# A Mamba-2 mixer with a gated stream mixer: pieces for the norm multiply, CB one slot later, and another order at both ends of the output passes

## The reference, cut to what matters

```python
xn = _layernorm(x)
# the mixer
proj = einsum('bld,pd->blp', xn, in_proj_w)        # gate 4096, x/B/C 6144, dt 64
xBC = silu(conv4(hbc) + conv_bias)                  # causal, 4 taps
dt_p = softplus(dt + dt_bias); A = -exp(A_log)
state = state * exp(dt_p * A) + dtx * B             # 64 heads in 8 groups, 128 states
y = state . C + x * D
var = mean(y * y over the 512 channels of a group)
yn = y * rsqrt(var + EPS) * norm_weight * silu(gate)
s = einsum('bli,di->bld', yn, out_proj_w)           # 4096 -> 1024
# the stream mixer
H_res = sinkhorn_log(logits, 50 iterations)         # 4 x 4 per token, also H_pre, H_post by softmax
g = silu(H_res . streams + (H_pre . streams) @ W_branch * H_post)
out = x + s * g
```

## Time and profile before

| | |
|---|---|
| median of 3 runs | 3083.32 us |
| the profiled execution | 3077.91 us |
| its span, first to last instruction | 3076.4 us |
| VectorE busy | 2177.6 us, 71% |
| ScalarE busy | 1744.7 us, 57% |
| GpSimd busy | 644.8 us, 21% |
| matmuls | 14304 |
| mean granted TensorE clock | 0.996 of full speed |

### The profile page before, as it was taken

One profiled execution on the slowest core, in us unless ns is written; L12 is line 12 of the kernel. 1 busy time (PEld: TensorE's weight loads), 2 busy tenths in 40 slices (PEclk: granted clock), 3 DMA queues, 4 the chain that ended last, 5 costly groups with the idle time before them and its releaser, 6 DMA issues.

```text
span 3076.4 us, 45008 instructions
## 1 busy us (share of the span) xinstructions
PE 3006.5 (98%) x14304; PEld 2340.5 (76%) x14304; DVE 2177.6 (71%) x2660; ACT 1744.7 (57%) x3716; POOL 644.8 (21%) x447
## 2 busy tenths in 40 slices
PE   7999999999999998999999999999998999999998
PEld 6777777777777777777777777777776888887786
DVE  7667576676757687767676766767666878677877
ACT  3576575757566575576575757576675232234443
POOL 3322212121212234312222121222223000001112
PEclk9999999999999999999999999999999999999999
DMA  3434343333424353435243433334354444456665
GB/s 129 169 126 151 104 159 117 140 116 130 154 102 161 104 185 118 155 120 178 99 166 106 157 106 140 132 114 154 110 175 129 141 138 150 144 195 209 215 205 178
DMA packets 125528, 444.86 MB, mean 145 GB/s; under 512 B 17488, under 2 KB 21712, under 8 KB 109008
## 3 DMA queue, kind: packets, MB, share of 16 engines
q1 hardware_dynamic: 117552, 423.14, 41.0%
q0 software_dynamic: 4096, 14.68, 1.2%
q10 hardware_dynamic: 3744, 5.51, 0.5%
HBM read 397.86 MB, written 45.42 MB: 144 GB/s over the span
## 4 chain that ended last, share of the span: by engine, by line
PE 84%; DVE 6%; issue 6%; DMA 2%; ACT 2%; POOL 0%; SPq 0%; DVEq 0%; ACTq 0%; POOLq 0%
PE bank L1069 17%; PE bank L1071 17%; PE bank L1070 17%; PE bank L1107 8%; PE bank L1301 6%; PE bank L1302 6%; PE bank L1303 6%; PE bank L1081 2%; DVE acc L803 1%; PE bank L1093 1%; PE bank L1117 1%; DVE xbc L815 1%; DVE w_lo L785 1%; DMA acc<-in_w_out 1%; DMA units<-cum_scratch 1%
## 5 line engine op out<-in xcount | busy, mean ns | idle before, releaser
L1069 PE MATMUL bank<-x_hi,w_hi 128*128 128x512 f32 x2560 | 1023.9, 400 | 9.3 <-DVE acc L803 9.3
L1071 PE MATMUL bank<-x_hi,w_lo 128*128 128x512 f32 x2560 | 999.4, 390 | 0.0
L1070 PE MATMUL bank<-x_lo,w_hi 128*128 128x512 f32 x2560 | 997.3, 390 | 0.0
L803 DVE SCALAR_TENSOR_TENSOR acc<-bank,conv_w,acc 128x511 f32<-128x511 f32 (+2 forms) x576 | 430.7, 748 | 303.2 <-ACT acc L602 275.8
L1069 PEld LDWEIGHTS bank<-x_hi,w_hi 128*128 128x128 f32 x2560 | 480.6, 188 | 127.9 <-issue 23.1
L1071 PEld LDWEIGHTS bank<-x_hi,w_lo 128*128 128x128 f32 x2560 | 480.5, 188 | 104.2
L1070 PEld LDWEIGHTS bank<-x_lo,w_hi 128*128 128x128 f32 x2560 | 481.3, 188 | 93.6
L602 ACT ACTIVATE acc<-bank,tap_par 128x512 f32<-128x512 f32 x192 | 149.2, 777 | 579.7 <-PE bank L1071 434.1
L1301 PE MATMUL bank<-x_hi,w_hi 128*128 128x512 f32 x1024 | 402.5, 393 | 19.9 <-DVE x_lo L1293 15.6
L1302 PE MATMUL bank<-x_lo,w_hi 128*128 128x512 f32 x1024 | 400.4, 391 | 0.0
L1303 PE MATMUL bank<-x_hi,w_lo 128*128 128x512 f32 x1024 | 400.2, 391 | 0.0
(11 more groups left out here) (154 smaller groups left out, 3388.2 us busy)
## 6 DMA issues: line engine op xcount, KB each, us to landing
units<-cum_scratch SPq DMA_DIRECT2D x128, 1280.0 KB, 6.8
w_raw<-in_w_in SPq DMA_DIRECT2D x160, 512.0 KB, 3.7
w_raw<-y_scratch SPq DMA_DIRECT2D x128, 512.0 KB, 3.6
y_scratch<-gate SPq DMA_DIRECT2D x32, 1024.0 KB, 6.6
acc<-in_w_out SPq DMA_DIRECT2D x128, 256.0 KB, 3.8
xbc<-in_x SPq DMA_DIRECT2D x16, 512.0 KB, 6.3
units<-in_x SPq DMA_DIRECT2D x16, 512.0 KB, 3.7
rstd_b<-rc_scratch SPq DMA_DIRECT2D x32, 256.0 KB, 4.1
```

What stands on the lines that cost most here:

```text
L803: dve.scalar_tensor_tensor(acc[:, s % 2, back:], bank_proj[s % 2][:, 0:SEQ - back], mix.conv_w[:, at, m, 3 - back:4 - back], acc[:, s % 2, ...
L1069: pe.matmul(out, w_hi[m % 2][:, k, :], hi, start=(k == 0), stop=False)
L1070: pe.matmul(out, w_hi[m % 2][:, k, :], lo, start=False, stop=False)
L1071: mm = pe.matmul(out, w_lo[m % 2][:, k, :], hi, start=False, stop=(k == KT - 1))
```

## The change

It has four parts and some renaming.

1. `scale` issues four instructions of 512 elements, one a channel tile, where it issued one of 2048; only the last raises the semaphore.
2. In `LATER` and `LAST` the scores (`cb`) stand in slots 5 and 7, which stood in 4 and 6, and so their mask products (`bc`) in 6 and 8.
3. The step into the output passes. k tiles 2 and 3 get buffers of their own (`pair`, in parts of `x_hi` and `x_lo` that are free by then), and all later ones use these; so the splits of k tiles 2 and 3 no longer wait for `k_done` (`reused`). TensorE takes k tile 0 for five banks, then the multiply of unit 7, then k tile 1 for five banks, then the column sums. ScalarE splits k tile 1 before the last but two squares, k tile 2 before the last square. VectorE weighs unit 7 before it splits k tile 1, splits k tile 2 after `finish_y`, and does the first part of the guarded iteration (`guard_rows`, `guard_row_sums`) and the split of k tile 3 around the two variances, the rest behind them. Its tables move from `sums` to `dtx`, since `sums` is still in use.
4. The last k tile of the last pass: TensorE takes k tile 30 for five token tiles, then k tile 30 and 31 in turn, the latter five token tiles behind, and raises `bank_done` for each bank; VectorE multiplies a bank when its own count is reached.

The renaming joins semaphores (`lv_done` and `ln_rstd_done` into `ln_step`, `z_done` into `dt_step`) and shifts the counts; the number of waits is as before.

```diff
-LATER = Plan(cb=[4, 6], load=[4, 5, 7, 10, 12, 14, 16, 18], mult=[9, 11, 13, 15, 17, 19, 21, 23],
+LATER = Plan(cb=[5, 7], load=[4, 5, 7, 10, 12, 14, 16, 18], mult=[9, 11, 13, 15, 17, 19, 21, 23],
...
-LAST = Plan(cb=[4, 6], load=[4, 5, 7, 10, 12, 14, 15, 17], mult=[9, 11, 13, 14, 16, 18, 20, 21],
+LAST = Plan(cb=[5, 7], load=[4, 5, 7, 10, 12, 14, 15, 17], mult=[9, 11, 13, 14, 16, 18, 20, 21],
...
-            part = gate[:, :, q * SEQ:(q + 1) * SEQ]
             pool.wait_ge(rstd_loaded[q], 16 * (g + 1))
             pool.wait_ge(gated, UNITS * g + UNITS - SEQS + q + 1)
-            pool.tensor_tensor(part, part, rstd_b[:, q, :].unsqueeze(1).to_broadcast([P, XT, SEQ]),
-                               ALU.mult).then_inc(scaled, 1)
+            for c in range(XT):
+                part = gate[:, c, q * SEQ:(q + 1) * SEQ]
+                op = pool.tensor_tensor(part, part, rstd_b[:, q, :], ALU.mult)
+            op.then_inc(scaled, 1)
...
+            if ends_all(half, plan) and s == SLOTS - 1:
+                output.split_hi(act, 0, 0, 1)
...
-        act.wait_ge(proj_done, SLOTS * HALVES * GROUPS)
-        output.split_hi(act, 0, 0, 1)
-        drain(piece, HALVES - 1)
+        drain(piece, HALVES - 1, SLOTS, LAST.square[-1])
+        output.split_hi(act, 0, 1, 0)
+        drain(piece, HALVES - 1, LAST.square[-1])
...
+        drain(last_piece, HALVES - 1, SLOTS, LAST.mult[-1])
         output.split_lo(dve, 0, 0, 1)
-        drain(last_piece, HALVES - 1)
+        drain(last_piece, HALVES - 1, LAST.mult[-1], min(LAST.var))
+        output.split_lo(dve, 0, 1, 0)
...
-        drain(piece, HALVES - 1, SLOTS, SLOTS + 1)
+        drain(piece, HALVES - 1, SLOTS, LAST.mult[-1])
         pe.wait_ge(bc_done, SEQS * HALVES * GROUPS)
         pe.wait_ge(gate_taken, GATE_SLOTS * HALVES * GROUPS)
-        first_products((3, 4, 7, 0, 1))
-        drain(piece, HALVES - 1, SLOTS + 1, SLOTS + 3)
+        first_products(0, (3, 4, 7, 0, 1))
+        drain(piece, HALVES - 1, LAST.mult[-1], LAST.norm[0])
+        first_products(1, (3, 4, 7, 0, 1))
+        drain(piece, HALVES - 1, LAST.norm[0], LAST.norm[1])
         pe.wait_ge(y_done, UNITS * HALVES * GROUPS)
-        first_products((5, 6))
-        drain(piece, HALVES - 1, SLOTS + 3)
+        for j in range(2):
+            first_products(j, (5, 6))
+        drain(piece, HALVES - 1, LAST.norm[1])
...
+    def pair(self, p, i):
+        return 0 if p == 0 and isinstance(i, int) and i == 0 else 1
+
+    def reused(self, p, i):
+        return not (p == 0 and isinstance(i, int) and i < 2)
...
-        need(act, self.k_done, kk - 1)
-        act.activation(self.y_hi[j], self.y_raw[:, j, :], ACT.Copy)
-        act.activation(self.w_hi[j], self.w_raw[:, j, :], ACT.Copy).then_inc(self.k_hi, 1)
+        if self.reused(p, i):
+            act.wait_ge(self.k_done, kk - 1)
+        n = self.pair(p, i)
+        act.activation(self.y_hi[n][j], self.y_raw[:, j, :], ACT.Copy)
+        act.activation(self.w_hi[n][j], self.w_raw[:, j, :], ACT.Copy).then_inc(self.k_hi, 1)
...
+        guard_rows()
+        last_variance(dve, 0)
+        guard_row_sums()
+        one(0, 1, 1)
+        last_variance(dve, 1)
+        guard_columns()
+        guard_column_sums()
+        for n in range(SK_AHEAD):
+            iterate(n)
...
-        dve.wait_ge(k_done, OT * PASSES)
         dve.wait_ge(s_mul, ROWS)
         for t in range(NT):
+            dve.wait_ge(bank_done, t + 1)
...
+        pe.wait_ge(output.k_split, OT * PASSES - 1)
+        for t in range(NT + LAG):
+            if t < NT:
+                output.product(pe, PASSES - 1, OT // 2 - 1, 0, t)
+            if t == LAG:
+                pe.wait_ge(output.k_split, OT * PASSES)
+            if t >= LAG:
+                output.product(pe, PASSES - 1, OT // 2 - 1, 1, t - LAG, last=True).then_inc(bank_done, 1)
```

More of the change, by code:

```diff
@@ L1234, in step, with first_products @@
                     piece(*group)
-        def first_products(tiles, last=False):
-            for j in range(2):
-                output.products(pe, 0, 0, j, tiles, first=(j == 0), done=last)
+        def first_products(j, tiles, last=False):
+            output.products(pe, 0, 0, j, tiles, first=(j == 0), done=last)
         for half in range(HALVES):
@@ L1299, in products, with output_programs @@
                 pe.wait_ge(self.evacuated[t % 2], NT // 2 * (p - 1) + t // 2 + 1)
-            toks = slice(t * P, (t + 1) * P)
-            pe.matmul(self.bank[t][:, :], self.y_hi[j][:, toks], self.w_hi[j], start=first, stop=False)
-            pe.matmul(self.bank[t][:, :], self.y_hi[j][:, toks], self.w_lo[j], start=False, stop=False)
-            mm = pe.matmul(self.bank[t][:, :], self.y_lo[j][:, toks], self.w_hi[j], start=False, stop=last)
+            mm = self.product(pe, p, i, j, t, first, last)
         if done:
             mm.then_inc(self.k_done, 1)
-def output_programs(nc, ctx, core, mix, output, all_stored):
+def output_programs(nc, ctx, core, mix, output, all_stored, last_variance):
     d = core.dram
@@ L1409, in run_sync @@
                 all_stored(sp)
-            k_steps(sp, p, one, done=3)
+            k_steps(sp, p, one, begin=3)
         def load_tile(n, i, p, part):
```

148 lines of the change are left out of this document (78 added, 70 removed).

## The result

The changed kernel takes **3057.54 us** (median of 4 runs, 3056.92 to 3058.41), the kernel before beside it 3083.02 (4 runs, 3082.41 to 3083.66): 25.5 us less, a ratio of 0.9918, 95% interval 0.9900 to 0.9935. The forecast was 3058.4. That it was met so closely is luck: up to the output passes the changed kernel gained 5.7 us less than forecast, the medians lie 5.7 us further apart than the two traces, and the two errors cancelled. Only the traces show this.

A forecast was written before the change was run, and what follows sets the result against it. TensorE, busy 98% of the span, was taken as the bound, with only its waits to win. Terms 10.4 + 1.6 + 1.4 + 1.3 + 8.2 + 2.0 = 24.9 us off the 3083.3 median gave 3058.4 us, range 3049 to 3067.

The forecast's parts named there:

- A: Group loop: four-piece norm multiply frees the silu, ending 13 TensorE waits for the convolution; 10.4 us gained, bounds 7 and 11.4.
- B: Second group of each half: the two waits for `weigh` go too; 1.6 us gained, bounds 0 and 1.6.
- D: Between the halves: pieces let the first split end earlier, shortening TensorE's wait; 1.3 us gained, bounds 0.5 and 1.6.
- C: Score matmuls a slot later: neutral for TensorE, only `weigh` waits for them; 1.4 us gained, bounds 0 and 1.4.
- R4: Rival, loop: mask product between silu and convolution becomes the new wait, 2.4 us lost a group, time 3091; chance 0.03.
- a wait for the mask: Sign that the prediction is wrong: TensorE's waits in the loop show one for the mask or `weigh`; no size given.
- E: Step into the output passes: new order and buffers shorten waits, k tile 5 starts earlier; 8.2 us, bounds 4 and 14.
- the 0.8 subtracted for half rate: Output step: allowance, somewhat less than half of 1.9 us, for half rate possibly following the new wait before k tile 5.
- R1: Rival: the output step hardly gains, SP's order setting k tile 5; step gain about 3, time 3063.6 us; chance 0.14.
- R3: Rival: k tile 5 in time, no half rate; step gains 14, end gains 3, time 3051.6 us; chance 0.12.
- F: Kernel's end: last multiplies start earlier, limited by VectorE's free time and GpSimd's adds; 2.0 us, bounds 1 and 3.1.
- 5.4 above the profiled one; the gain is the same: Final sum: carries the 24.9 us gain from the profiled execution, 3077.9, to the median of runs, 3083.3, giving 3058.4.

The follow-up runs named there:

- the third trace: The kernel before, unchanged, profiled once more after the second trace: 3084.55 us (one run), span 3083.0.
- the second trace: The kernel before, unchanged, profiled again: 3084.84 us (10 runs), ratio 1.0006, span 3090.5.
- the other order on SP: Changed kernel with SP's loads of k tiles 4 and 5 ahead of both stores, k tile 6's between them: 3056.63 us, ratio 0.9917.
- one multiply: Changed kernel with the norm multiply in one instruction per sequence again, scores still in slots 5 and 7: 3056.93 us, ratio 0.9913.

## Why the prediction was right, and where it was not

*A, B and D* were right in mechanism and a little small: alone, the pieces give 16.3 us in the loop where A to D had 14.7. (A's upper bound adds up to 11.5 and not 11.4; nothing hangs on it.) There a group gained 1.0 to 1.2, forecast 0.92 with another 0.1 as a bound. The Trainium skill, "SBUF — State Buffer", section "Who interferes with whom", says that issue order and not the operation's shape decides who blocks; the traces agree, with 0.68 against 5.10 us for the same silu.

*C* was wrong, and its sign too. The step that failed is "Who waits for them is `weigh`": the second scores wait as well, for the banks that the first mask product frees. The prediction put this mask product behind the convolution of slot 6 and did not ask whether it still ends before slot 7's scores; the time that the column sums had given it was gone. Forecast 1.4 gained, measured 5.1 lost up to the first output product once the pieces are there (some 0.53 in each of ten groups). The rival R4 had the mask product as the new wait, but ahead of the convolution and for several us; it does not describe this. The prediction's own sign of being wrong, "a wait for the mask" in the loop, is there, and by it this part of the mechanism fell although the time came out.

*What A and C share* was missed: the later scores were taken as neutral for the blocked silu. Alone they remove that wait too, by way of SP's queue, so the change holds two remedies for one wait and pays for the second.

*E* was 8.2 forecast and is 8.2 against the trace that it was worked out from, 10.5 against the third trace. The working holds in the main when it is counted from the first output product (2333.91 before, 2324.88 now). TensorE ends k tile 3 at 30.2 (forecast 2364, that is 30.1) and starts k tile 5 at 39.1 (forecast 2374.3, that is 40.4). The load of k tile 5 is issued at 28.4, and was at 29.3: held in place, as taken. Missed were that k tile 4 comes 1.8 late by itself, and that k tile 6 waits 1.9, its load queued behind the second store; the 0.8 subtracted for half rate covered part of it, and no half rate came. So k tile 5 gained 10.4 us where 9.0 was forecast, 2.2 of that were lost behind it where 0.8 had been subtracted, and that both sums give 8.2 is in part luck. R1 was too low, R3 too high.

*F* was 2.0 forecast, 2.2 measured, by the mechanism given: VectorE's free moment bounds the start, GpSimd's adds the end.

*The sum* went wrong in the sentence "5.4 above the profiled one; the gain is the same". It is not: the gain is 25.5 us in the medians and 19.8 in the traces, 5.7 apart. The profiled execution was a short one in several places at once. Against the third trace, whose span of 3083.0 is near the median's, the changed kernel's is 26.4 us shorter. The places where this exceeds the 19.8 are those of the table above: the first half's end and front, the step, the other products and the end. The race in the last group is none of them, for the silu was first in both traces; the changed kernel, whose longest silu is 1.75 us, can no longer lose the 5.0 us of the second trace there. Why the other places vary stays open. The loop's shortfall is 14.7 - 9.0 = 5.7. The two cancel, and 3058.4 met 3057.5 by that much luck.

## What to carry to other kernels

Before an instruction is moved, list every wait on what it produces and on what it frees, on all engines, and every queue whose next entry waits for its neighbours: here a mask product freed banks for the next scores, and a split released the DMA that set when GpSimd starts. Where two engines block each other for whole instructions, cut the longer one down until whoever waits has its margin back (half the length was enough here), and measure that alone before adding another remedy: the pieces alone gave 20.7 us of the 25.5. One trace of a kernel whose executions vary is one throw of the dice. Compare the profiled time with the median before a gain is carried from the one to the other, and look for pairs of instructions that start within 0.1 us of each other; but a second and a third trace showed here that such a pair was only one of several places.

## What was unexpected of the hardware

- A start order of 0.02 to 0.07 us decides between 0.68 and 5.1 us for one instruction, and with it over 2 to 5 us of the kernel (last group 142.0 with the silu first; 144.2 or 146.9 with the multiply first).
- Convolutions, which read one operand from PSUM, run at full speed beside the multiply (21 of the 576 in the trace shown first lie wholly within one, and the longest of them takes 0.75, as elsewhere), while splits, silus and adds with both operands in SBUF are held.
- Much the same idle of TensorE before the same matmul was followed by a granted clock of 1.00 in one trace (1.21 us idle, the changed kernel), 0.58 in another (1.23, the other order on SP) and 0.57 in a third (1.22, one multiply). Which of the two comes was not settled by any run, and part of the scatter between executions stays with it.
